# A graph network kernel on one core: the running column maximum by one tensor_reduce per chunk

## The reference

```
h = max(layernorm(x), 0)
x = x + tanh([h, t] @ W1 + b1) @ W2 + b2 + adj @ (h @ B.T) - rowsum(adj) * (h @ B.T)
h = max(layernorm(x), 0);  feats = (h @ W) in 8 heads of 8
scores[h,i,j] = leaky_relu(a_self[i,h] + a_neigh[j,h]) - 1e10 * (1 - adj[i,j])
x = x + relu(softmax_j(scores) @ feats + bias)
```

## Time and profile before

| what | value |
|---|---|
| runs | 914.73, 913.28, 913.76 us, median 913.76 |
| span of the profiled execution, first to last instruction | 911.1 us |
| the profiled execution's own time | not listed apart; the runs' median, 913.76, stands for it |
| PE busy | 778.1 us |
| DVE busy | 732.2 us |
| DMA | 281.57 MB, mean 309 GB/s |

### The profile page before, as it was taken

How to read it: one execution, slowest core, us unless ns; L and a number is a source line. 1 busy time by engine, 2 the same in 40 slices (tenths; PEclk the granted TensorE clock), 3 DMA queues, 4 the chain that set the end, 5 groups by cost and what they waited for, 6 DMA issues and landing times.

```text
span 911.1 us, 13284 instructions
## 1 busy us (share of the span) xinstructions
PE 778.1 (85%) x5222; PEld 266.2 (29%) x5222; DVE 732.2 (80%) x958; ACT 129.5 (14%) x212; POOL 152.6 (17%) x145
## 2 busy tenths in 40 slices
PE   3688999999999999999999999999999999950000
PEld 1223333333333332323233333333333333320000
DVE  1799996989898989898998989898989898962111
ACT  1234111111111010201111111111111111110000
POOL 1210110202020202020202020101101020217775
PEclk9889999999999999999999999999999999985555
DMA  9958779797979798897979797979797979601121
GB/s 367 367 198 305 286 272 428 280 428 283 430 297 414 319 392 356 354 394 317 414 296 419 291 420 292 418 293 422 290 426 285 428 282 427 273 9 40 48 60 42
DMA packets 37266, 281.57 MB, mean 309 GB/s; under 512 B 14336, under 2 KB 18560, under 8 KB 20736
## 3 DMA queue, kind: packets, MB, share of 16 engines
q1 hardware_dynamic: 31408, 276.83, 74.7%
q0 software_dynamic: 4096, 4.20, 1.8%
q10 hardware_dynamic: 1744, 0.28, 0.2%
HBM read 277.10 MB, written 4.19 MB: 309 GB/s over the span
## 4 chain that ended last, share of the span: by engine, by line
PE 72%; DVE 9%; POOL 7%; issue 5%; DMA 4%; ACTq 2%; ACT 1%; POOLq 0%; DVEq 0%; SPq 0%
PE acc L722 42%; PE row_sums L730 22%; POOL gathered L349 7%; DMA ring<-in_adj_t 3%; DVE max_hi L510 2%; ACTq L367 2%; PE ps_hid L750 1%; PE ps_feat L792 1%; DVE pstat L478 1%; PE ps_xb L771 1%; PE ps_acc L764 1%; DVE max_lo L509 1%; PE ps_turn L778 1%; PE ps_acc L769 1%; PE ps_acc L767 1%
## 5 line engine op out<-in xcount | busy, mean ns | idle before, releaser
L722 PE MATMUL acc<-ring,x_pb 128*64 128x512 f32 x2048 | 461.2, 600 | 14.6 <-DMA ring<-in_adj_t 14.1
L509 DVE TENSOR_TENSOR max_lo<-max_lo,ring 128x2048 f32<-128x2048 f32 x96 | 219.7, 2288 | 44.3 <-DMA ring<-in_adj_t 43.8
L730 PE MATMUL row_sums<-ring,ones_cols 128*32 128x512 f32 x2048 | 243.3, 604 | 13.4 <-DVE x_pb L495 13.4
L722 PEld LDWEIGHTS acc<-ring,x_pb 128*64 128x64 f32 x2048 | 140.6, 138 | 322.6 <-issue 321.9
L510 DVE TENSOR_TENSOR max_hi<-max_hi,ring 128x2048 f32<-128x2048 f32 x96 | 219.2, 2284 | 0.0
L340 POOL DMA_INDIRECT cand<-in_adj,cls_row x64 | 78.0, 1219 | 695.0 <-DVE cls_row L539 680.4
L730 PEld LDWEIGHTS row_sums<-ring,ones_cols 128*32 128x32 f32 x2048 | 56.8, 110 | 166.6 <-issue 150.6
L349 POOL DMA_INDIRECT gathered<-feats_dram,best x64 | 63.2, 988 | 19.5 <-issue 19.5
L647 DVE TENSOR_TENSOR gathered<-gathered,bias_row 128x512 f32<-128x512 f32 x8 | 5.5, 692 | 68.1 <-DMA gathered<-feats_dram,best 68.1
L506 DVE TENSOR_TENSOR max_hi<-ring 128x2048 f32<-128x2048 f32 x16 | 36.6, 2291 | 6.5 <-DMA ring<-in_adj_t 6.3
L504 DVE TENSOR_TENSOR max_lo<-ring 128x2048 f32<-128x2048 f32 x16 | 36.7, 2292 | 2.4 <-DMA ring<-in_adj_t 0.5
(11 more groups left out here) (95 smaller groups left out, 418.6 us busy)
## 6 DMA issues: line engine op xcount, KB each, us to landing
ring<-in_adj_t SPq DMA_DIRECT2D x128, 2048.0 KB, 10.2
x_tq<-in_x SPq DMA_DIRECT2D x1, 2048.0 KB, 35.1
feats_dram<-feats SPq DMA_DIRECT2D x16, 128.0 KB, 2.3
out<-gathered SPq DMA_DIRECT2D x8, 256.0 KB, 2.2
x_pb<-in_x SPq DMA_DIRECT2D x1, 1536.0 KB, 7.8
cand<-in_adj,cls_row POOLq DMA_INDIRECT x64, 6.1
gathered<-feats_dram,best POOLq DMA_INDIRECT x64, 2.4
x_pb<-in_x SPq DMA_DIRECT2D x1, 512.0 KB, 4.6
```

Source lines behind the costliest of these rows:

```text
L509: dve.tensor_tensor(max_lo[:, :], max_lo[:, :], lo, ALU.max).then_inc(lo_done, 1)
L722: last = pe.matmul(acc[parity][at:at + D, :], x_pb[:, c * CB + b, :], slot(c)[:, b * W:(b + 1) * W], start=(c == 0 and b < 2), stop=(c == ...
L730: last = pe.matmul(row_sums[at:at + QUAD, :], ones_cols[:, :], slot(c)[:, b * W:(b + 1) * W], start=(c == 0 and b < 4), stop=(c == NC - 1 ...
```

## The change

VectorE's folding is rewritten. Each ring slot grows from 8 blocks to 9 (`SLOT` = 9 x 512): the ninth, `spare`, carries the running maximum. Chunk 0 is folded by one `tensor_reduce` over its eight blocks, which writes its 512 maxima into the spare block of chunk 1's slot. Chunks 1 to 6 are folded by one `tensor_reduce` over nine blocks, their own eight and the spare one, into the spare block of the next slot; chunk 7's goes to `runmax`. The reduce runs over the view `p (b i) -> p i b` (`by_row`): for each of 512 columns i it reads 8 or 9 words that lie 512 words (2048 bytes) apart, and writes one. The buffers `max_lo` and `max_hi`, `fold_maxima` and three semaphores go; one semaphore `max_done` stands for all. The wait for `runmax_turned` moves from before the fold to before chunk 7's reduce. The general path, which does not run here, uses a free part of the ring.

```diff
--- before.py
+++ after.py
@@ -37,7 +37,7 @@
 CB = 8
 NC = NB // CB
 RING = 4
-HALF = CB * W // 2
+SLOT = (CB + 1) * W
 QUAD = 32
 FA = D + 2 * HEADS
 EPS = 1e-5
@@ -67,15 +67,13 @@
 
 
 
-        ring = sb("ring", [P, RING * CB * W])
+        ring = sb("ring", [P, RING * SLOT])
         gathered = sb("gathered", [P, NB, D])
         ones_cols = sb("ones_cols", [P, QUAD])
         h_t = sb("h_t", [P, N])
         x_pb = sb("x_pb", [P, NB, D])
         x_tq = sb("x_tq", [P, NB, D])
         feats = sb("feats", [P, NB * FA])
-        max_lo = sb("max_lo", [P, HALF])
-        max_hi = sb("max_hi", [P, HALF])
         cand = sb("cand", [P, TB, NB])
         hidden = sb("hidden", [HID, W])
         acc_sb = sb("acc_sb", [P, W])
@@ -152,9 +150,7 @@
         pro_h = sem("pro_h")
         chunk_in = [sem(f"chunk_in{r}") for r in range(RING)]
         pe_chunk = sem("pe_chunk")
-        lo_done = sem("lo_done")
-        hi_done = sem("hi_done")
-        fold = sem("fold")
+        max_done = sem("max_done")
         hid_ready = sem("hid_ready")
         hid_done = sem("hid_done")
         strip_h_done = sem("strip_h_done")
@@ -172,7 +168,6 @@
         feat_ready = sem("feat_ready")
         feat_done = sem("feat_done")
         feat_stored = sem("feat_stored")
-        runmax_done = sem("runmax_done")
         runmax_turned = sem("runmax_turned")
         cls_top = sem("cls_top")
         cls_done = sem("cls_done")
@@ -227,7 +222,14 @@
                      ps_acc[0:D, :, :]]
 
         def slot(n):
-            return ring[:, (n % RING) * CB * W:(n % RING + 1) * CB * W]
+            return ring[:, (n % RING) * SLOT:(n % RING) * SLOT + CB * W]
+
+        def spare(n):
+            return ring[:, (n % RING) * SLOT + CB * W:(n % RING + 1) * SLOT]
+
+        def by_row(n, first, blocks):
+            at = (n % RING) * SLOT
+            return ring[:, at + first * W:at + (first + blocks) * W].rearrange("p (b i) -> p i b", b=blocks)
 
         def wide(a, k, n=D):
 
@@ -247,7 +249,7 @@
             def load(s, c):
 
                 sp.wait_ge(pe_chunk, s * NC + (c - RING + 1))
-                sp.wait_ge(hi_done, s * NC + (c - RING + 1))
+                sp.wait_ge(max_done, s * NC + (c - RING + 1))
                 sp.sem_inc(sp_past, 1)
                 src = adj_t[bass.ds(s * NC + c, 1)].rearrange("a p f -> (a p) f")
                 sp.dma_start(slot(c), src).then_inc(chunk_in[c % RING], 16)
@@ -497,29 +499,15 @@
 
             def fold_chunk(s, c):
 
-                n = s * NC + c
                 dve.wait_ge(chunk_in[c % RING], s * (16 * NC // RING) + 16 * (c // RING + 1))
-                lo, hi = slot(c)[:, 0:HALF], slot(c)[:, HALF:2 * HALF]
                 if c == 0:
-                    dve.tensor_tensor(max_lo[:, :], lo, hi, ALU.max).then_inc(hi_done, 1)
-                elif c == 1:
-                    dve.tensor_tensor(max_hi[:, :], lo, hi, ALU.max).then_inc(hi_done, 1)
+                    dve.tensor_reduce(spare(c + 1), by_row(c, 0, CB), AX.X, ALU.max).then_inc(max_done, 1)
+                elif c < NC - 1:
+                    dve.wait_ge(max_done, s * NC + c)
+                    dve.tensor_reduce(spare(c + 1), by_row(c, 0, CB + 1), AX.X, ALU.max).then_inc(max_done, 1)
                 else:
-                    dve.wait_ge(hi_done, n)
-                    dve.tensor_tensor(max_lo[:, :], max_lo[:, :], lo, ALU.max).then_inc(lo_done, 1)
-                    dve.tensor_tensor(max_hi[:, :], max_hi[:, :], hi, ALU.max).then_inc(hi_done, 1)
-
-            def fold_maxima(s):
-
-                dve.wait_ge(hi_done, s * NC + NC)
-                dve.wait_ge(lo_done, s * (NC - 2) + NC - 2)
-                dve.tensor_tensor(max_lo[:, :], max_lo[:, :], max_hi[:, :], ALU.max).then_inc(fold, 1)
-                dve.wait_ge(fold, s * 2 + 1)
-                dve.tensor_tensor(max_lo[:, 0:2 * W], max_lo[:, 0:2 * W], max_lo[:, 2 * W:4 * W], ALU.max)\
-                    .then_inc(fold, 1)
-                dve.wait_ge(fold, s * 2 + 2)
-                dve.tensor_tensor(runmax[:, :], max_lo[:, 0:W], max_lo[:, W:2 * W], ALU.max)\
-                    .then_inc(runmax_done, 1)
+                    dve.wait_ge(max_done, s * NC + c)
+                    dve.tensor_reduce(runmax[:, :], by_row(c, 0, CB + 1), AX.X, ALU.max).then_inc(max_done, 1)
 
             def search_classes(s):
 
@@ -587,8 +575,9 @@
 
             def strip(s):
 
-                dve.wait_ge(runmax_done, s)
                 for c in range(NC):
+                    if c == NC - 1:
+                        dve.wait_ge(runmax_turned, s)
                     fold_chunk(s, c)
                     if c == 3:
                         search_classes(s - 1)
@@ -597,9 +586,6 @@
                         scale_h1(s - 1)
                     if c == 6:
                         search_candidates(s - 1)
-                dve.wait_ge(runmax_turned, s)
-                fold_maxima(s)
-
             for g in range(NC + 1):
                 if g < NC:
                     centre(g)
@@ -611,7 +597,6 @@
                     variance(g)
             constants()
             fold_chunk(0, NC - 1)
-            fold_maxima(0)
             dve.wait_ge(x_b2_done, 1)
             with dve.Fori(1, S) as s:
                 strip(s)
@@ -685,7 +670,7 @@
                         dve.tensor_scalar(gap[:, 1, 0:1], gap[:, 0, 0:1], -1.0, None, ALU.mult).then_inc(gen_max, 1)
                         for g in range(NB // 4):
                             dve.wait_ge(gen_p_turned, n * (NB // 4) + g + 1)
-                            dve.tensor_copy(max_lo[:, (g % 2) * W:(g % 2 + 1) * W], acc[g % 2][:, :])\
+                            dve.tensor_copy(ring[:, 2 * N + (g % 2) * W:2 * N + (g % 2 + 1) * W], acc[g % 2][:, :])\
                                 .then_inc(gen_p_copied, 1)
                         dve.wait_ge(gen_exp, n + 1)
                         dve.reciprocal(gap[:, 3, 1:2], gap[:, 2, 0:1]).then_inc(gen_chain, 1)
@@ -773,7 +758,7 @@
                 last.then_inc(acc_turned, 1)
 
             def turn_maxima(s):
-                pe.wait_ge(runmax_done, s + 1)
+                pe.wait_ge(max_done, s * NC + NC)
                 for k in range(TB):
                     last = pe.transpose(ps_turn[:, k * P:(k + 1) * P], runmax[:, k * P:(k + 1) * P], ident[:, :])
                 last.then_inc(runmax_turned, 1)
@@ -862,8 +847,8 @@
                             pe.wait_ge(gen_p_copied, n * (NB // 4) + g + 1)
                             for k in range(4):
                                 j = g * 4 + k
-                                at = (g % 2) * W + k * P
-                                last = pe.matmul(ps_hid[:, 0:HD], max_lo[:, at:at + P],
+                                at = 2 * N + (g % 2) * W + k * P
+                                last = pe.matmul(ps_hid[:, 0:HD], ring[:, at:at + P],
                                                  feats[:, bass.ds(h * HD + j * FA, HD)],
                                                  start=(j == 0), stop=(j == NB - 1))
                         last.then_inc(gen_sum, 1)
```

## The result

The changed kernel takes 1320.12 us (median of 4 runs, 1319.83 to 1320.43), the kernel before 914.22: a ratio of 1.444, interval [1.4419, 1.446]. I had forecast 1329.

A forecast was written before the change was run, and what follows sets the result against it. TensorE bounds the kernel before; after the change VectorE sets the strip. Strip 1 starts at 121.8 us, plus 15 x 73.3 makes 1221, plus 105.6 for the end makes 1327 of span; runs lie 2.66 above, so 1329 us, range 912 to 1470.

The forecast's parts named there:

- TensorE sets the strip, with 3.5 us of cover on VectorE: Loop before the change: TensorE takes 47.55 us per strip, VectorE 44.07, leaving 3.5 us of cover.
- The rate: VectorE's new reduces: 1.75 ns per scattered word, 8.21 us for 4608 elements; 1.6 to 1.87 ns had 46%.
- the full rate: VectorE's scattered reads keep 1.04 ns: 914.8 us if hidden (22%), 919 us with a tie that shows (12%).
- 1.98: VectorE's reduces: ns per word if scattering adds to the engine's pace; 1463 us; two cycles or nearly had 13%.
- the first rival: VectorE's reduces keep 1.04 ns and its 47.5 us strip hides inside TensorE's 47.55; 914.8 us, chance 22%.
- The strip: Loop: VectorE needs 64.8 us of folding, 8.4 of other work and 0.1 for starts, 73.3 us per strip.
- Strip 0: Before the loop's later strips: longer folds and one more turn of normalising make strip 1 start at 121.8 us.
- The hold: Strip 0: GpSimd's L331, starting at 39.41 and lasting 8.86 us, blocks VectorE's L478; unblocked, strip 1 starts 8.7 us earlier.
- The end: After the last strip: transposes, search and 64 fetches take 105.6 us, none of which changes.
- The clock rival: TensorE's granted clock stays at 0.50 because of its gaps, a strip takes 95 us; 1627 us, chance 3%.
- Loads, store, semaphores, moved wait: Loop: none limits; DMA share falls from 0.86 to 0.56, loads come in time, and VectorE hardly waits for chunks.

The follow-up runs named there:

- step table: The changed kernel with a different step between the words of one result in each chunk, 2 to 512 words; 1276.55 us.
- runs table: The changed kernel with chunks 1 to 4 and 6 reducing 8 words per result in runs of adjacent words with a hop between; 1041.96 us.
- the run with a quiet TensorE: The changed kernel with TensorE doing 2 of 8 products per chunk and sums of half of chunk 0 only, loads kept; 1291.19 us.

## Why the prediction was right, step by step

- *TensorE sets the strip, with 3.5 us of cover on VectorE.* Right: with the reads side by side the strip grew by 0.28 us only, with VectorE's folding at 4.41 + 7 x 4.95.
- *The rate.* 1.75 ns per scattered word, taken from ScalarE's writes. Measured (8143 - 144) / 4608 = 1.736 for L507 and 1.757 for L510, 1.77 for L504. This step carried everything, and it was lent from another engine and from the other direction. It was a choice at 46 in 100, and the full rate, at 34, was the only other large one. The step table and the runs table show that the cost is that of a word taken alone from its 16 bytes; 1.98 is refuted for a single stream, and so is the first rival, by which a single read stream would keep 1.04 ns. That the time is that of a memory port is the reading that fits two engines of different pace, and no run shows a port; the 0.23 ns of a second stream do not fit ports that are wholly apart. Some luck is in the size: with TensorE standing, a word takes (7875 - 144) / 4608 = 1.68 ns, and TensorE's disturbance, which the prediction did not have, brought the mean to 1.74. By my sum, at 5.8 us for 0.01 ns, 1.68 is 1288 us, where the run with a quiet TensorE took 1291. And the range, 912 to 1470, held nearly every rival; that 1320 lies in it says little, that it lies in 1300 to 1370 says more.
- *The strip.* 73.3 predicted, 72.7 measured: x15 this is -9 us, the largest error. Half of it is folding, 64.5 us for my 64.8, the other half the rest of VectorE's work, 8.2 for 8.5. Within the folding two errors nearly cancel: in chunks 3 and 4 TensorE waits and the reduce takes 7.88, 0.33 less than my 8.21, which is 0.66 of a strip, and the other six together take 0.36 more. That TensorE's activity enters into it I had not foreseen.
- *Strip 0.* Strip 1 starts at 119.8 us, 121.8 predicted. The hold ended at 47.3, not 48.3, since the add began earlier; that is one of the two. The other lies in the work between the folds, 14.0 us from there on for my 14.8.
- *The end.* From the end of the last `runmax` (1202.3 + 7.96 = 1210.3) to 1318.8 it is 108.5 us, 105.6 predicted. I had said that none of it changes. TensorE's transposes there take 1.12 us for 0.66: they now follow a wait of 6.11 us, and the granted clock is 0.50 in the 1.3 us before them and 0.55 in the work behind them, where it was 1.00 before. VectorE gets its sums 5.5 us after `runmax` where it was 3.4, which is 2.2 of the 2.9 us:

```profile
1210.31 1.12 PE L763 MATMUL ps_turn<-ident,runmax 128*128 128x128 f32 x4 [6.11 <-DVE runmax L510]
...
1215.79 0.42 DVE L552 TENSOR_TENSOR tmp<-ps_xb,acc_tq 128x256 f32<-128x256 f32 x1 [5.53 <-ACT acc_tq L422]
```

- -9, -2 and +2.9 make -8.1, and 1327 - 8.1 is the measured span of 1318.8 within a microsecond.
- *The clock.* It fell in each gap (0.50 in the stretch from 375.87 to 383.66) and recovered; the mean granted clock was 0.815 for 0.936. It cost TensorE in the loop, where it had time to spare, and the kernel only at the end, the 2.2 us above. The clock rival (1627 us) did not occur. (The prediction took the first three slices of the page for all of strip 0; it reaches into the fourth, which reads 0.9.)
- *Loads, store, semaphores, moved wait.* No wait of VectorE for a chunk appears in the loop; right.

## What to carry to other kernels

Before a view is rearranged on a busy engine, ask how many words it takes from each 16 bytes. Two are enough for the full rate, 1.04 ns for a 4-byte element; a word alone costs 1.7 to 1.85 ns, and the near steps of 16 and 32 bytes cost the most. `tensor_tensor` compares two words per step where `tensor_reduce` takes in one, so this fold in halves (35.7 us a strip) is even a little cheaper than the reduce at its best (39.1). When a long instruction on GpSimd stops VectorE, look at what stands beside it in its new place before you move it: beside a `tensor_reduce` it held nothing, beside a `tensor_tensor` it held 8.7 us. If there is no such place, cut it up.

## What the hardware showed that was not expected

- TensorE at work lengthens VectorE's scattered reads by up to 6% (7.87 to 8.37 us) and its side-by-side reads not at all (4942 to 4954 ns). The loads show no such effect (7.88 us at DMA shares of 0.73 and of 0.21).
- A step of 8 bytes is free and one of 16 bytes the dearest of all (8.66 us), dearer than 2048 bytes (8.27 in the same chunk).
- A GpSimd `tensor_tensor` of 8.8 to 10.7 us holds a VectorE `tensor_scalar` (7.86 us for 0.17) and also a VectorE `tensor_tensor` with both sources in SBUF (10.95 for 2.28), but not a `tensor_reduce` (8.32 us beside it, within the 7.87 to 8.37 of the others). A `tensor_tensor` on VectorE holds GpSimd's in turn: 1.95 us for 0.73.
